# One block for norm and front, a 128-row step projection, silu(z) and gating moved forward, and two mixer batches joined

## The chip, the cores and the metric

The kernel runs on one core of a Trainium2 chip. The metric is the device time of one execution in microseconds (us). Engines are named as in the profile: PE (TensorE; PEld its weight loads), DVE (VectorE), ACT (ScalarE), POOL (GpSimd) and SP (SyncE, which issues the DMAs here). They run their own instruction streams in order and meet at semaphores.

## The reference

Four layers work on x, 1024 tokens (4 batches of 256) by 512 values, each with a layer norm before, a layer norm after and a residual add. They are a selective scan, a layer of experts with low-rank parts, a 128-head mixer with causal convolution, and a gated FFN. The change touches the first and the third. The first is, cut:

```python
proj = hidden_states @ in_proj_w            # 512 -> 2 x 1024
x, z = jnp.split(proj, 2, axis=-1)
xc = silu(conv4(x) + conv_b)                # causal, 4 taps
ssm_p = einsum('bdl,ed->ble', xc, x_proj_w) # 64 rows: 32 step, 16 B, 16 C
dt_r, Bm, Cm = (rmsnorm(part) for part in ssm_p)
dt = softplus(einsum('blr,dr->bdl', dt_r, dt_proj_w) + dt_bias)
ys = _selective_scan(xc, dt, -exp(A_log), Bm, Cm)
y = (ys + D_param[None, :, None] * xc) * silu(z)
return einsum('bdl,hd->blh', y, out_proj_w)
```

The third projects to 18,560 columns, convolves, and forms for each head and batch a kernel of decays times C.B products, which is multiplied with the head's values (two heads share a pair of 128 rows).

## The kernel before, in words

Stages follow one another as blocks; every engine meets the others at a block's end. Products of full precision are done as three fp32r matmuls of high and low parts (`mm3`, lines 78 to 80): high by high, high by low, low by high.

`first_norm` (L175) is the first block after the one that loads constants. SP loads the eight 128-token tiles of x; DVE waits for all of them, takes the statistics (L201, L204), and after ACT's root (L219) normalizes (L208). PE turns each tile (L230), ACT copies the high part (L222), DVE subtracts for the low part (L213).

`scan_front` (L234) is the second block. SP loads `w_in0` in eight slices of 256 columns (L280) and six tables (L286); POOL splits each slice (L300, L302). PE does 32 `proj` steps of 12 matmuls of 128x512 on three banks: the first 16 are x, two per 128 channels (one for each half of the tokens), the last 16 are z. An x step is followed by ACT's first tap (L441), three taps on DVE (L382), ACT's Silu (L447) and one `x_proj` matmul (L326) three steps later. A z step is copied by DVE (`z_copy`, L390). Once x is done, the 64 rows are squared (L457), summed by matmul (`sums`, L334), rooted (L460), inverted (L404) and scaled (L406). Then come 16 `steps` (L342), plain f32 matmuls of 32 rows on two banks, two between each pair of z steps. ACT takes Abs (L465) and Exp (L469) and, after all, Ln (L472); DVE takes the relu (L395) and the last sum (L433).

`selective_scan` (L475) runs 128 units in order: 8 `kk` (two channel tiles and one half of the tokens) of 16 states `n`. In a unit, PE makes the inputs (L689, 16 matmuls), ACT the decay (L551), DVE scans (L608), POOL multiplies by C (L645), PE sums over states two units later (L700, 8 matmuls). The ring of scanned tiles and that of products hold three each. At n = 8 of the next `kk` DVE adds the skip (`skip`, L616), at n = 9 it makes dt times x (L600), at n = 10 PE turns that (L659).

`out_proj_and_norm` (L721): ACT takes Silu of z in place in eight parts (L871), DVE multiplies it into y (`gated`, L932), ACT and DVE split y (L880, L937), ACT and POOL split the weights (L875, L791), and PE multiplies: four pairs of channel tiles, then four token tiles. `gated(6)` and `gated(7)` stand among the norm's statistics (L941 and on).

`mixer_groups` (L1374) runs eight groups of nine steps: step 0 of a group projects B and C, steps 1 to 8 each project a pair of heads (four `proj` of 12 matmuls, each in two parts), while PE does the pair before: it turns the pair's values (`turn`, L1612) and multiplies them with the kernels (`y_mm`, L1629 and L1633, one call per batch b = 0 to 3). Kernels are made by ACT (L1930, L1931 clamps; L1943, L1949 exponentials) and DVE (L1754), eight per pair in four buffers; `y_mm(p, 0)` frees two of them for kernels 4 and 5, `y_mm(p, 1)` for 6 and 7. Steps 1 to 4 of groups 1 to 7 also hold two `out_tile` calls of 24 matmuls each (outputs of the group before), whose input parts come from ACT (L1958) and DVE (L1795); steps 5 to 8 prepare weights for them (L1965, L1808).

PE's order within such a step is written by hand (L1673 on):

```python
turn(p, 0); proj(s, 0, 0); proj(s, 0, 1)
turn(p, 1); proj(s, 1, 0); proj(s, 1, 1)
y_mm(p, 0)
if outs: out_tile(*outs[0])
proj(s, 2, 0); proj(s, 2, 1)
y_mm(p, 1)
proj(s, 3, 0); proj(s, 3, 1)
if outs: out_tile(*outs[1])
y_mm(p, 2); y_mm(p, 3)
```

## Time and profile before

| | |
|---|---|
| Median of 3 runs | 2557.45 us (2557.25 to 2561.41) |
| The profiled execution | 2554.48 us, span 2552.7 us |
| Mean granted TensorE clock | 0.969 |
| Busy: PE, DVE, ACT, POOL | 93%, 72%, 59%, 48% of the span |

A busy share is that of instructions in execution, and PE's are pipelined, so a full PE row is not PE at its peak: what counts is the distance from one start to the next. A bracket behind an instruction is the idle time of its engine before it and what ended that. `x8` is a run of eight instructions of a kind.

### The profile page before, as it was taken

Reading aid. Unit: us, or ns where it says so; the run is one execution under the profiler, and the core shown is the slowest. Engines: PE = TensorE matmul, PEld = TensorE weight load, DVE = VectorE, ACT = ScalarE, POOL = GpSimd, SP = SyncE. Lnnn points to the kernel's source line nnn. Section 1 sums busy time; section 2 is a strip of 40 time slices with the busy share of each in tenths; the row PEclk is TensorE's granted clock in tenths of the full one; section 3 lists DMA queues with packets and bytes.
Section 4 is the critical chain, followed back from the end, with each engine's and each line's share of the span. In section 5 each row is a group of like instructions: output and inputs, shape, how many; then the busy total and the mean of one; then the engine's idle time right before and its main releaser. Section 6 shows DMA issues by size and latency. Waiting matters only on the chain. (4 is left out here: it accounts for less than half of the span.)

```text
span 2552.7 us, 38270 instructions
## 1 busy us (share of the span) xinstructions
PE 2371.1 (93%) x13836; PEld 1916.2 (75%) x13836; DVE 1840.2 (72%) x3052; ACT 1504.5 (59%) x3201; POOL 1213.3 (48%) x782
## 2 busy tenths in 40 slices
PE   5979999977669999999999999999999999779997
PEld 4559999976456777777777777777777777569996
DVE  4558888875548866966966857857857867697777
ACT  2365585553338956857857867857758668632221
POOL 1228888864224734634625724724635535432212
PEclk9989999998879999999999999999999999899999
DMA  2010020021023412312312213313223223201100
GB/s 83 26 67 2 1 67 1 1 71 34 34 86 107 124 50 82 116 51 82 111 54 94 97 58 99 96 53 102 90 66 99 80 64 100 90 26 50 47 30 34
DMA packets 108540, 167.42 MB, mean 66 GB/s; under 512 B 9488, under 2 KB 77456, under 8 KB 107328
## 3 DMA queue, kind: packets, MB, share of 16 engines
q1 hardware_dynamic: 108352, 164.97, 20.2%
q8 instruction: 111, 1.82, 0.3%
q14 instruction: 77, 0.63, 0.1%
HBM read 158.58 MB, written 6.36 MB: 65 GB/s over the span
## 5 line engine op out<-in xcount | busy, mean ns | idle before, releaser
L78 PE MATMUL mg_pb<-xTh,mg_wh 128*128 128x512 f32 x1152 | 479.5, 416 | 8.1 <-PEq L1296 8.1
L1544 POOL TENSOR_TENSOR mg_y<-mg_hT,mg_sg 128x512 f32<-128x512 f32 x128 | 187.7, 1467 | 598.1 <-DVE mg_hT L1779 598.1
L79 PE MATMUL mg_pb<-xTl,mg_wh 128*128 128x512 f32 x1152 | 454.0, 394 | 0.0
L80 PE MATMUL mg_pb<-xTh,mg_wl 128*128 128x512 f32 x1152 | 452.4, 393 | 0.0
L1727 DVE SCALAR_TENSOR_TENSOR mg_hT<-mg_pb,mg_cw,mg_hT 128x510 f32<-128x510 f32 (+2 forms) x432 | 319.0, 743 | 23.2 <-ACT mg_hT L1899 14.6
L608 DVE TENSOR_TENSOR_SCAN o<-ss_da,ss_dbx 128x1024 f32<-128x1024 f32 x128 | 291.7, 2284 | 51.8 <-PE ss_dbx L689 49.3
L1754 DVE TENSOR_TENSOR mg_m<-mg_gb,mg_cb 128x384 f32<-128x384 f32 x512 | 265.7, 550 | 71.5 <-ACT mg_gb L1949 68.2
L78 PEld LDWEIGHTS mg_pb<-xTh,mg_wh 128*128 128x128 f32 x1152 | 217.2, 189 | 67.2 <-issue 27.6
L689 PE MATMUL ss_dbx<-ss_diag,ss_uT 128*128 128x128 f32 x2048 | 253.0, 277 | 7.7 <-DVE o L608 6.9
L80 PEld LDWEIGHTS mg_pb<-xTh,mg_wl 128*128 128x128 f32 x1152 | 217.4, 189 | 51.3
L551 ACT ACTIVATE ss_da<-dt,ss_na 128x510 f32<-128x510 f32 x256 | 170.3, 714 | 144.6 <-DVE o L608 144.5
L689 PEld LDWEIGHTS ss_dbx<-ss_diag,ss_uT 128*128 128x128 f32 x2048 | 241.2, 194 | 10.2 <-DVE o L608 8.9
L79 PEld LDWEIGHTS mg_pb<-xTl,mg_wh 128*128 128x128 f32 x1152 | 218.0, 189 | 38.5
L645 POOL TENSOR_TENSOR ss_pr<-o,ss_c 128x1024 f32<-128x1024 f32 x86 | 206.4, 2400 | 35.9 <-PE ss_zT L700 32.9
L1949 ACT ACTIVATE mg_gb<-mg_nd 128x256 f32<-128x256 f32 x512 | 189.7, 371 | 54.7 <-DVE mg_nd L1772 54.7
L1943 ACT ACTIVATE mg_gb<-mg_abc,mg_tabs 128x128 f32<-128x128 f32 x512 | 183.2, 358 | 22.8 <-DVE mg_m L1754 21.9
L78 PE MATMUL mg_tb<-mg_wogh,mg_yh 128*128 128x512 f32 x448 | 180.0, 402 | 0.0
L1534 POOL TENSOR_TENSOR mg_wl<-mg_ws,mg_wh 128x1024 fp32r<-128x1024 f32 x71 | 175.1, 2466 | 5.9
L79 PE MATMUL mg_tb<-mg_wogl,mg_yh 128*128 128x512 f32 x448 | 177.1, 395 | 0.0
L80 PE MATMUL mg_tb<-mg_wogh,mg_yl 128*128 128x512 f32 x448 | 177.0, 395 | 0.0
L1629 PE MATMUL mg_py<-mg_m,mg_hc 128*64 128x256 f32 x1024 | 166.2, 403 | 9.2 <-DVE mg_m L1754 9.1
L1803 DVE SCALAR_TENSOR_TENSOR o<-mg_tb,mg_rs,o 128x512 f32<-128x512 f32 x56 | 41.8, 747 | 179.4 <-PE mg_tb L80 179.4
(323 smaller groups left out, 5370.4 us busy)
## 6 DMA issues: line engine op xcount, KB each, us to landing
mg_abc<-acs_rows SPq DMA_DIRECT2D x256, 256.0 KB, 3.4
mg_ws<-in_w_in SPq DMA_DIRECT2D x72, 512.0 KB, 3.7
mg_wos<-in_w_out SPq DMA_DIRECT2D x64, 256.0 KB, 3.7
ss_c<-c_rows SPq DMA_DIRECT2D x8, 1024.0 KB, 5.8
ff_ws<-in_w SPq DMA_DIRECT2D x7, 1024.0 KB, 4.9
x<-in_x SPq DMA_DIRECT2D x16, 256.0 KB, 4.4
ip_ws<-in_w_in SPq DMA_DIRECT2D x8, 512.0 KB, 3.5
ff_w2s<-in_w SPq DMA_DIRECT2D x7, 512.0 KB, 7.1
```

Source lines behind the costliest of these rows:

```text
L78: pe.matmul(out, lhs[0], rhs[0], start=start, stop=False)
L79: pe.matmul(out, lhs[0], rhs[1], start=False, stop=False)
L80: return pe.matmul(out, lhs[1], rhs[0], start=False, stop=stop)
L608: dve.tensor_tensor_scan(hh[i % RH], da[i % 2][:], dbx[i % 2][:], 0.0, ALU.mult, ALU.add).then_inc(s_h, 1)
L645: pool.tensor_tensor(pr[i % RP], two(hh[i % RH]), crow[:, n, :].unsqueeze(1).to_broadcast([P, 2, HALF]), ALU.mult).then_inc(s_pr, 1)
L689: ins = pe.matmul(dbx[i % 2][:, a * HALF + m * P:a * HALF + (m + 1) * P], uT[kk % 2][:, a, m, :], diag[:, n, m, :], start=True, stop=True)
L1534: pool.tensor_tensor(wl[s % 2][:], ws[:], wh[s % 2][:].bitcast(F32), ALU.subtract).then_inc(s_lo, 1)
L1544: pool.tensor_tensor(yb[:, p % RING, t], hT[s % 2][:, t], sg[s % 2][:, t], ALU.mult).then_inc(s_y2, 1)
L1727: i = dve.scalar_tensor_tensor(out=d3, in0=s3, scalar=w[:, TAPS - 1 - k:TAPS - k], in1=d3, op0=ALU.mult, op1=ALU.add)
L1754: dve.tensor_tensor(mm[u % 4][:], gb[u % 2][:, 0:BLK], cbt[:, u // 2, :], ALU.mult).then_inc(s_m, 1)
L1943: act.activation(gb[u % 2][:, 2 * P:BLK], abc[(BATCH * p + b) % 3][:, hh, P:SEQ], ACT.Exp, bias=tabs[g % 2][:, 2, 2 * b, 2 * q + hh:2 * q ...
L1949: act.activation(gb[u % 2][:, 0:2 * P], nd[u % 4][:], ACT.Exp, scale=1.0 if by_dve(p, b) else -1.0).then_inc(s_e, 1)
```

## The change

1. `first_norm` goes; its work is done inside `scan_front`'s block, in two halves of four token tiles. SP loads four tiles of x, the first weight slice, the other four tiles, the second slice, then seven tables. PE turns four tiles, does `proj(0)` (which needs the first half of the tokens only), turns the other four and goes on with `proj(1)`.
2. The step projection becomes one fp32r matmul of 128 rows. The rows are B, C and the 32 step rows three times; `x_proj` now gives 128 rows instead of 64. `bch` holds high parts, with low parts in the last 32 rows; `dph` holds the projection's high part, with its low part in rows 64 to 95. POOL makes `dph` before slice 4, ACT copies `bch` high (two Copy), DVE subtracts (two). `steps` uses four banks and goes in groups of four, each followed by one z step; the turning of B moves behind the first group.
3. z steps 0 to 8 leave their bank through ACT's Silu; z steps 9 to 15 are copied by DVE and get Silu in place at the block's end. All Exp come after all Abs.
4. Gating leaves `out_proj_and_norm`: POOL gates the `kk` before at n = 11 of `kk` 1 to 7 in the scan, DVE the last one after the last skip.
5. In the mixer `y_mm(p, 0)` and `y_mm(p, 1)` stand together, behind the first `out_tile` and ahead of `proj(s, 2, 0)`.

Core of the diff:

```diff
+    TH = MT // NH
+    Z_ACT, GROUP = 9, 4
...
+        dph = sb(c, "sp_dph", [R, DIN], F32R)
+        bch = sb(c, "sp_bch", [R, TOK], F32R)
+        dp, p0, sq = (sz[:, CD // 2 + i, :] for i in range(3))
-        pd = banks(c, "sp_pd", 2)
+        pd = banks(c, "sp_pd", 2) + pp
+        x = dt[:, 0:CD // 2, :].rearrange("p k (a d) -> p (k a) d", d=DM)
+        h0 = sz[:, 0:CD // 2, :].rearrange("p k (a d) -> p (k a) d", d=DM)
...
+                def load_x(h):
+                    for m in range(h * TH, (h + 1) * TH):
+                        sp.dma_start(x[:, m, :], x_tok[:, m, :]).then_inc(s_x[h], 16)
+                load_x(0)
                 load(0)
+                load_x(1)
                 load(1)
-                for t, n in ((cw, "conv_w0"), (cb, "conv_b0"), (xp, "x_proj"), (dp, "dt_proj"), (db, "dt_bias0"),
-                             (lw, "ln_w0")):
-                    sp.dma_start(t[:], I[n]).then_inc(s_tab, 16)
+                for t, n in ((cw[:], "conv_w0"), (cb[:], "conv_b0"), (xp[:], "x_proj"), (dp, "dt_proj"), (db[:], "dt_bias0"),
+                             (lw[:], "ln_w0"), (blk[:], "norm_blocks")):
+                    sp.dma_start(t, I[n]).then_inc(s_tab, 16)
...
+                def dt_weights():
+                    pool.wait_ge(s_tab, 112)
+                    pool.wait_ge(s_lo, 4)
+                    pool.tensor_scalar(dph[:], dp, 1.0, 0.0, ALU.mult, ALU.add).then_inc(s_dph, 1)
+                    pool.wait_ge(s_dph, 1)
+                    pool.tensor_tensor(dph[2 * RNK:3 * RNK, :], dp[2 * RNK:3 * RNK, :],
+                                       dph[2 * RNK:3 * RNK, :].bitcast(F32), ALU.subtract).then_inc(s_dph, 1)
+                    pool.wait_ge(s_dph, 2)
                 for s in range(CD):
+                    if s == 4:
+                        dt_weights()
...
+                def turn_x(m):
+                    pe.wait_ge(s_h0, m + 1)
+                    if m >= len(pd):
+                        pe.wait_ge(s_x0lo, m - len(pd) + 1)
+                    for k in range(KD):
+                        i = pe.transpose(pd[m % len(pd)][:, k * P:(k + 1) * P], h0[:, m, k * P:(k + 1) * P], ident)
+                    i.then_inc(s_t0, 1)
                 def proj(n):
...
+                    if n < 2:
+                        pe.wait_ge(s_x0lo, (n + 1) * TH)
                     if n >= 3:
-                        if n - 3 < NT:
+                        z = n - 3 - NT
+                        if z < 0:
                             pe.wait_ge(s_cv, n - 2)
+                        elif z < Z_ACT:
+                            pe.wait_ge(s_sz, z + 1)
                         else:
-                            pe.wait_ge(s_sz, n - 3 - NT + 1)
+                            pe.wait_ge(s_zc, z - Z_ACT + 1)
...
                 def steps(n):
                     k, h = divmod(n, 2)
-                    pe.wait_ge(s_bcn, h + 1)
-                    if n >= 2:
-                        pe.wait_ge(s_rl, n - 1)
-                    pe.matmul(pd[n % 2][:], dp[:, k * P:(k + 1) * P], bcn[0:RNK, half(h)], start=True, stop=True
+                    pe.wait_ge(s_bcl, h + 1)
+                    if n == 0:
+                        pe.wait_ge(s_dph, 2)
+                    if n >= len(pd):
+                        pe.wait_ge(s_rl, n - len(pd) + 1)
+                    elif n >= 2:
+                        pe.wait_ge(s_cp, n - 1)
+                    pe.matmul(pd[n % len(pd)][:], dph[:, k * P:(k + 1) * P], bch[:, half(h)], start=True, stop=True
                               ).then_inc(s_pd, 1)
...
+                for m in range(TH):
+                    turn_x(m)
+                proj(0)
+                for m in range(TH, MT):
+                    turn_x(m)
+                for n in range(1, NT):
                     proj(n)
...
-                done = 0
-                for n in range(NT + 5, 2 * NT):
-                    for i in range(done, min(done + 2, NT)):
+                for n in range(NT // GROUP):
+                    for i in range(n * GROUP, (n + 1) * GROUP):
                         steps(i)
-                    done = min(done + 2, NT)
+                    if n == 0:
+                        turn_b()
+                    proj(NT + 5 + n)
+                for n in range(NT + 5 + NT // GROUP, 2 * NT):
                     proj(n)
-                for i in range(done, NT):
-                    steps(i)
-                for m in range(MT):
-                    i = pe.transpose(pq[:, m * R:(m + 1) * R], bcn[:, m * P:(m + 1) * P], cst[0:R, C_ID:C_ID + R])
-                i.then_inc(s_bt, 1)
...
+                for h in range(NH):
+                    norm_x(h)
+                    for m in range(h * TH, (h + 1) * TH):
+                        x_low(m)
+                dve.wait_ge(s_tab, 112)
                 for n in range(NT):
                     taps(n)
-                z_copy(0)
                 copied(0)
-                z_copy(1)
                 copied(1)
-                z_copy(2)
                 normed(0)
                 normed(1)
-                z_copy(3)
-                z_copy(4)
-                done = 0
-                for n in range(5, NT):
-                    for i in range(done, min(done + 2, NT)):
-                        relu(i)
-                    done = min(done + 2, NT)
+                for h in range(NH):
+                    r = slice(3 * RNK, R)
+                    dve.wait_ge(s_bch, h + 1)
+                    dve.wait_ge(s_bcn, h + 1)
+                    dve.tensor_tensor(bch[r, half(h)], bcn[r, half(h)], bch[r, half(h)].bitcast(F32), ALU.subtract
+                                      ).then_inc(s_bcl, 1)
+                for n in range(NT):
+                    relu(n)
+                    if n == GROUP - 1:
+                        dve.wait_ge(s_bt, 1)
+                        dve.tensor_copy(bt[:], pq[:, 0:MT * RNK].rearrange("p (m r) -> p m r", r=RNK)[:, :, 0:NST]
+                                        ).then_inc(s_dt, 1)
+                for n in range(Z_ACT, Z_ACT + 4):
                     z_copy(n)
-                for i in range(done, NT):
-                    relu(i)
-                dve.wait_ge(s_bt, 1)
-                dve.tensor_copy(bt[:], pq[:].rearrange("p (m r) -> p m r", r=R)[:, :, RNK:RNK + NST]).then_inc(s_dt, 1)
-                for k in range(CD):
-                    dve.wait_ge(s_ln, k + 1)
-                    dve.tensor_tensor(dt[:, k, :], dt[:, k, :], rl(k), ALU.add).then_inc(s_dt, 1)
+                step_sum(0)
+                z_copy(13)
+                step_sum(1)
+                step_sum(2)
+                z_copy(14)
+                step_sum(3)
+                z_copy(15)
+                for k in range(4, CD):
+                    step_sum(k)
...
+                def z_silu(n):
+                    k, h = divmod(n, 2)
+                    act.wait_ge(s_proj, NT + n + 1)
+                    act.activation(sz[:, k, half(h)], pb[(NT + n) % 3][:], ACT.Silu).then_inc(s_sz, 1)
...
+                for h in range(NH):
+                    root_x(h)
+                    for m in range(h * TH, (h + 1) * TH):
+                        x_high(m)
...
                 silu(NT - 1)
-                for h in range(NH):
-                    act.wait_ge(s_cp, h + 1)
-                    act.activation(sq[:, half(h)], p0[:, half(h)], ACT.Square).then_inc(s_sq, 1)
+                z_silu(0)
+                squares(0)
+                z_silu(1)
+                squares(1)
+                z_silu(2)
...
+                for h in range(NH):
+                    act.wait_ge(s_bcn, h + 1)
+                    act.activation(bch[:, half(h)], bcn[:, half(h)], ACT.Copy).then_inc(s_bch, 1)
+                z_silu(3)
+                z_silu(4)
...
+                    act.activation(dt[:, k, half(h)], pd[n % len(pd)][:], ACT.Abs, bias=db[:, k:k + 1]).then_inc(s_abs, 1)
+                    if n % GROUP == GROUP - 1:
+                        z_silu(5 + n // GROUP)
...
+                    act.activation(dt[:, k, :], dt[:, k, :], ACT.Exp, scale=-1.0).then_inc(s_exp, 1)
+                for k in range(CD):
+                    act.wait_ge(s_exp, k + 1)
                     act.activation(dt[:, k, :], dt[:, k, :], ACT.Ln, bias=eps[:, 3:4]).then_inc(s_ln, 1)
+                for n in range(Z_ACT, NT):
+                    k, h = divmod(n, 2)
+                    act.wait_ge(s_zc, n - Z_ACT + 1)
+                    act.activation(sz[:, k, half(h)], sz[:, k, half(h)], ACT.Silu).then_inc(s_zs, 1)
...
                 skip(KB - 1)
-                dve.wait_ge(s_fin, 2 * KB)
+                for a in range(2):
+                    k = tiles(KB - 1).start + a
+                    dve.wait_ge(s_fin, 2 * KB - 1 + a)
+                    dve.tensor_tensor(xc[:, k, tokens(KB - 1)], xc[:, k, tokens(KB - 1)], sz[:, k, tokens(KB - 1)],
+                                      ALU.mult).then_inc(s_gv, 1)
+                dve.wait_ge(s_gv, 2)
...
+                    if n == GATE_AT and kk:
+                        xv = xc[:, tiles(kk - 1), tokens(kk - 1)]
+                        pool.wait_ge(s_fin, 2 * kk)
+                        pool.tensor_tensor(xv, xv, sz[:, tiles(kk - 1), tokens(kk - 1)], ALU.mult).then_inc(s_gp, 1)
...
-                silu(0)
-                silu(1)
-                for j in range(HT):
+                high(0)
+                weights_high(0)
+                high(1)
+                for j in range(1, HT):
                     weights_high(j)
-                    high(j)
-                    if j < 3:
-                        silu(2 * j + 2)
-                        silu(2 * j + 3)
+                high(2)
+                high(3)
                 high(4)
...
-                gated(0)
-                gated(1)
                 for j in range(HT):
                     low(j)
-                    gated(j + 2)
...
-                    if m < 2:
-                        gated(6 + m)
...
                         proj(s, 1, 0)
                         proj(s, 1, 1)
-                        y_mm(p, 0)
                         if outs:
                             out_tile(*outs[0])
+                        y_mm(p, 0)
+                        y_mm(p, 1)
                         proj(s, 2, 0)
                         proj(s, 2, 1)
-                        y_mm(p, 1)
                         proj(s, 3, 0)
```

## Rows read from the trace of the kernel before

**Rows 1.** Busy time of stages; columns: stretch, length, busy (instructions), clock, DMA, GB/s.
```profile
98.50:164.50 66.00, 64.54 (x231) 39.74 (x230) 32.32 (x38) 34.60 (x39) 6.85 (x4) 1.00 0.03 9
...
183.30:551.70 368.40, 355.89 (x3176) 352.66 (x3175) 310.77 (x151) 207.08 (x367) 306.97 (x128) 1.00 0.06 19
...
790.00:2190.00 1400.00, 1385.19 (x7324) 1052.33 (x7324) 1025.16 (x1831) 1024.30 (x2326) 687.02 (x489) 1.00 0.27 85
```
**Rows 2.** Timeline, first norm to first projection; columns: start, length, engine, line, instruction.
```profile
3.37 3.65 SPq L194 DMA_DIRECT2D x<-in_x  x8
...
12.27 4.85 DVE L201 BATCH_NORM_STATS2 n_st<-x 128x6 f32<-128x512 f32 x8 [11.32 <-DMA x<-in_x]
...
18.40 3.74 DVE L208 TENSOR_SCALAR n_h<-x,n_mv,n_rs 128x512 f32<-128x512 f32 x8
...
20.15 0.60 ACT L222 ACTIVATE xTh<-n_tb 128x512 fp32r<-128x512 f32 x1 [2.02 <-PE n_tb L230]
...
22.05 4.89 DVE L213 TENSOR_TENSOR xTl<-n_tb,xTh 128x512 fp32r<-128x512 f32 x8
...
34.32 0.80 PE L78 MATMUL ip_pb<-xTh,ip_wh 128*128 128x512 f32 x1 [9.02 <-POOL ip_wl L302]
```
**Rows 3.** Timeline of ACT, DVE and PE, second half of the front.
```profile
108.44 0.77 ACT L460 ACTIVATE sp_sq<-sp_pq,eps,cst 64x512 f32<-64x512 f32 x1 [1.30 <-PE sp_pq L334]
...
116.66 0.88 DVE L406 SCALAR_TENSOR_TENSOR sp_bcn<-sp_p,sp_lw,sp_sq 64x512 f32<-64x512 f32 x1
...
150.76 1.98 PE L342 MATMUL sp_pd<-sp_bcn,sp_dp 32*128 32x512 f32 x4
...
154.58 1.28 ACT L472 ACT_TABLE_LOAD   x1
...
155.87 8.43 ACT L472 ACTIVATE dt<-dt,eps 128x1024 f32<-128x1024 f32 x8
...
158.45 0.69 DVE L390 COPY sz<-ip_pb 128x512 f32<-128x512 f32 x1 [2.03 <-PE ip_pb L80]
...
169.27 4.63 DVE L433 TENSOR_TENSOR dt<-dt,sp_rl 128x1024 f32<-128x1024 f32 x4
```
**Rows 4.** Timeline of POOL and DVE, last units of the scan.
```profile
536.86 2.36 POOL L645 TENSOR_TENSOR ss_pr<-o,ss_c 128x1024 f32<-128x1024 f32 x1 [0.32 <-PE ss_zT L700]
...
541.23 2.29 DVE L608 TENSOR_TENSOR_SCAN o<-ss_da,ss_dbx 128x1024 f32<-128x1024 f32 x1 [0.37 <-PE ss_dbx L689]
```
**Rows 5.** Timeline of POOL and PE, output projection: its start, and one later wait.
```profile
557.14 2.34 POOL L791 TENSOR_TENSOR op_wl<-x,op_wh 128x1024 fp32r<-128x1024 f32 x1 [10.33 <-ACT op_wh L875]
...
560.71 0.76 PE L78 MATMUL op_b<-op_wh,op_yh 128*128 128x512 f32 x1 [10.49 <-DVE op_yl L937]
...
598.03 1.12 PE L852 MATMUL op_tb<-cst,o 128*128 128x128 f32 x4 [2.60 <-DVE o L961]
```
**Rows 6.** Timeline of DVE and PE, mixer, two kinds of step.
```profile
1115.96 1.29 DVE L1795 TENSOR_TENSOR mg_yl<-mg_y,mg_yh 128x256 fp32r<-128x256 f32 x2
...
1205.97 0.66 PE L1612 MATMUL mg_tb<-cst,mg_hT 128*128 128x128 f32 x4
...
1215.99 0.39 PE L80 MATMUL mg_pb<-xTh,mg_wl 128*128 128x512 f32 x1
...
1217.45 0.40 PE L79 MATMUL mg_pb<-xTl,mg_wh 128*128 128x512 f32 x1
...
1220.09 0.65 PE L1629 MATMUL mg_py<-mg_m,mg_hc 128*64 128x256 f32 x4
...
1220.79 0.60 PE L1629 MATMUL mg_py<-mg_m,mg_hc 128*64 128x256 f32 x4
...
1221.54 0.66 PE L1612 MATMUL mg_tb<-cst,mg_hT 128*128 128x128 f32 x4
...
1236.91 0.65 PE L1629 MATMUL mg_py<-mg_m,mg_hc 128*64 128x256 f32 x4 [0.37 <-DVE mg_m L1754]
...
1237.71 0.65 PE L1612 MATMUL mg_tb<-cst,mg_hT 128*128 128x128 f32 x4
```

182 lines of the change are left out of this document (85 added, 97 removed).

## The prediction, made before the change was run

> **What bounds the kernel now.** I read the busy times by stage first: PE is occupied for 1385 of the mixer's 1400 us, for 356 of 368 in the scan and for 64.5 of 66 in the second half of the front, all at the full clock level, 2.4 GHz [rows 1]. Then I read the timeline around each edited place. The start is different: PE waits until 34.32 for its first projection, behind one serial chain (x lands, statistics, root, normalize, turn, split, and only then the weights' own load and split) [rows 2]. At the front's end ACT is in its eight Ln until 164.30 and DVE in its last sums until 173.90, while PE has done its last z step [rows 3]. So the start and the end of the front are not PE's; nearly everything between is, and there an edit pays only if it shortens PE's list or a wait of PE.
>
> **1. Norm inside the front.** Eight x tiles are issued in 3.65 us from 3.37 and all are there at 12.27 [rows 2]. With four of them issued by 5.2, I take 8.6 for the first half (an estimate: half way between 3.37 and 12.27, plus 0.8 for what every load takes). From first statistic to first normalized tile eight tiles took 6.13 us (12.27 to 18.40), 4.85 of them statistics [rows 2]; four tiles save half of that and 0.3 of aggregates, so 3.4 us: 12.0. The first high part came 1.75 after that point (20.15 against 18.40 [rows 2]); the later ones follow PE's turns, 0.86 apart, and the low part ends 1.2 after its high part begins: the fourth is there at 12.0 + 1.75 + 2.6 + 1.2 = 17.6. Slice 0 is queued behind four tiles only and is split by then. So proj(0) starts near 17.8 instead of 34.32. But DVE works in order: the second half's statistics begin only at 17.7; 3.4 us to 21.1, four tiles normalized at 3.74/8 = 0.47 each by 23.0, four low parts of 4.89/8 = 0.61 [rows 2] from 23.2 to 25.7. proj(1) starts at 25.7 if PE turns at 2.4 GHz, at 27.4 if at 1.2; in before it followed proj(0), at 38.9. That is 11.5 to 13.2 us less. PE idles for about 1 us on each side of these turns, and the first 3.9 us of projection ran at the lower level in before; a new fall would cost 1 to 2 us. I take **-12.0**, ends -13.2 and -9.5. SP's queue is passed by nothing urgent: its two larger tables, 1.1 MB with the rest, stand behind slice 1 and are wanted at 26.
>
> **2. 128 rows in x_proj.** The 16 matmuls and two sums move the same 512 columns; only their weights have twice the columns. **+0.5**, ends 0 and +1.6 (0.1 each). POOL's extra pair before slice 4 (3.4 us) lies in its wait for PE, over 9 us for each slice: 0; without that cover it would delay proj(16) by 3.4.
>
> **3. Second half of the front.** Two f32 steps hold PE for 1.98 us [rows 3]. As fp32r they are two of the matmuls of which 12 make the 2.72 us (0.69 + 2.03) from one z copy to the next [rows 3], 0.227 each, so 16 steps shed 16 x 0.76 = 12 us of PE. What is late next, in the times of before: ACT must do z_silu(2), ready at 107.4, before it may load the root's table, so the first root starts 0.9 us after the 108.44 of [rows 3] and both inversions shift with it. The last scaling ends at 118.4 instead of 117.54 [rows 3]; then come one Copy and one subtraction of 0.6 each, so that steps 0 and 1 start at 119.2 and 120.0, and PE has idled 2.3 us. Behind these waits stand the z steps, and ACT's and DVE's queues behind theirs. The four groups are paced by PE (3.65 us) and by the relu (0.8 us each against four banks): z steps 5 to 8 end at 124.5, 128.7, 132.4 and 136.5, and seven more at 2.72 end at 155.5. ACT is last now: Silu 0.6, table 1.28, eight Exp 8.4, table 1.28, eight Ln 8.43 [rows 3], table 1.28, seven Silu 3.9: 136.6 + 25.2 = 161.8. DVE's sums (4.63 for four [rows 3]) end at 160.6. The block ended at 173.90: -12.1. If PE's level falls in the 2.3 us gap, as it did after 2.60 us idle, where four transposes took 1.12 us [rows 5], z step 5 and all behind it are up to 1.5 late. I take **-11.3**, ends -12.8 and -6.
>
> A table load is 1.28 us in the trace and the next ACT instruction starts 0.01 behind it (154.58, 155.87 [rows 3]). The Trainium skill, "ScalarE: Activation LUTs", What ACT_TABLE_LOAD costs, gives every switch a drain of about 1.38 us on top. By the page the three loads from the Exp on would end the block at 165.9 and the whole sum would be -21.4; this row shows no such gap.
>
> **4. Gates in the scan.** They are seven POOL instructions of the size of L645, 2.36 us [rows 4]. POOL repeats every 2.66, so the next product is up to 2.1 late and 0.3 is made good per unit. Behind it wait a scan (for the product three before) and PE's sum. Product 124 ended at 539.22 and scan 127 began at 541.23 [rows 4], a slack of 2.0; the sum comes later still. So a gate costs 0 to 0.2 in the middle, where I take 0 (2.36 each if the slack is gone). In the last `kk` only four units are left to catch up: 1.65 late. DVE's two gates come after the last skip, where nothing runs beside them: 2 x 0.65. Together **+2.95**, ends +1.3 and +17.8.
>
> **5. Output projection.** PE started at 560.71 on DVE's low part; the weights' low part was ready at 559.48 [rows 5]. Silu and gate are gone from in front of the first, the weights' load and split are not: **-1.1** (560.6 to 559.5), and the weights are late next. The two gates among the norm's statistics lay in DVE's waits for POOL: 0. Ends -3 and 0.
>
> **6. Mixer.** A lone y_mm costs 1.00 us: 1215.99 to 1217.45, less two matmuls of 0.23; the second of a pair costs 0.70, 1220.09 to 1220.79 [rows 6]. Joining sheds 0.30 of PE per pair of heads, 19.2 for 64. Not all of it counts. In the steps with weights (5 to 8) a loop of ACT exponentials, DVE kernels, taps and clamps back to ACT needs some 16.3 us. PE's own step is 15.57 (1205.97 to 1221.54); the next is 16.17, PE waiting 0.37 for DVE's kernel [rows 6]. What PE sheds in these steps it waits: 0. Steps 3 and 4, where PE never waits, save 0.6 per group, step 0 of the next group 0.3. Step 2 loses: `out_tile` comes first now and needs DVE's low part, ready at 1117.25 [rows 6], while PE arrives at 1116.7: +0.55 - 0.30. That is -0.65 per group and **-4.5** for seven. In the steps with outputs y_mm(p, 0) comes 5.6 us later, so kernels 4 and 5 start about 2 us later, and queued behind them on DVE is the low part of the second output tile: 1128.7 instead of 1126.7 in the step of these rows, still 1.2 us before PE wants it. Ends -19.2 and +10.
>
> **Sum.** -12.0 + 0.5 - 11.3 + 2.95 - 1.1 - 4.5 = -25.5. The profiled execution took 2554.5, 3.0 under the median of 2557.45, so 2529.0 in a profile and 2532.0 as a median.
>
> **The rivals.**
> A, 0.16: the new front waits more. PE's level falls in both gaps and the relu paces the groups: +3 and +3, 2538. For it: the new path passes ACT, DVE and PE twice. Against: most of PE's work there is covered by ACT's last 25 us.
> B, 0.10: the mixer pays every join, -19.2 instead of -4.5: 2517. For it: PE is idle for 1.1% of the stage [rows 1]. Against: the 0.37 [rows 6].
> C, 0.07: each gate stalls the scan in full, +16.5: 2548. Against: the slack of 2.0 [rows 4].
> D, 0.06: ACT's table loads hold more than their row; once more 1.28 for each of three is 3.8: 2536. It is the way of the page named above, and the row speaks against it.
> E, 0.05, the other side: in the 21 steps with outputs DVE's second low part comes after PE. Beyond its 1.2 us of slack each microsecond costs 21. All other parts give -21, so it turns the sum when the low part comes 2.2 us later than I count and is measurably slower from 2.45: at 2.5 it is 2563. Against: PE does 5.5 us of projection between kernel 5 and that tile.
> The forecast holds 0.56.
>
> **How the numbers follow.** The forecast's own spread is 2524 to 2540. With A, D and half of B the range is 2517 to 2545, 0.83 of the cases. About 0.2%, 5 us, can be told from no change. Slower is E beyond its point, 0.03; same is E's milder part, 0.02; all else is faster, 0.95.
>
> **What would show it.** proj(0) near 18, proj(1) near 26; the front's block ending near 150 with ACT's Silu last; step matmuls 0.23 apart and PE idle over 2 us before the first; scan units 2.66 apart after each gate; PE's first output matmul 1.9 us later behind the last scan; mixer steps 5 to 8 as long as before and steps 3 and 4 shorter by 0.3. It is wrong if the front saves under 18 us, if a gate opens a gap in PE, or if PE waits for a low part in every step with outputs.

## The result, and the profile after

The changed kernel takes **2521.61 us** (median of 4 runs, 2520.92 to 2523.64) where the kernel before took 2557.45 (4 runs as well; the table ahead says 3). The ratio is 0.9857, with a 95% interval from 0.9842 to 0.9871: 35.8 us less. In the profiled execution the span is 2519.0 us instead of 2552.7, 33.7 less. The forecast was 2532.0 with a range from 2517 to 2545. So the direction and the range were right, and the gain was 10 us larger than forecast, by misses of both signs, the largest of them in the mixer and around `x_proj`.

The page of the changed kernel, its first part:

```profile
span 2519.0 us, 38251 instructions
PE 2339.3 (93%) x13820; PEld 1925.9 (76%) x13820; DVE 1823.6 (72%) x3040; ACT 1511.1 (60%) x3213; POOL 1232.6 (49%) x791
```

The shares are those of before. Where the time went is seen only from places that both kernels have. The table has the start of the same instruction in both traces, and the shift so far; a difference between two shifts is what a stage gained in this pair of profiles.

| Place | Before | After | Shift | Stage gained | Forecast |
|---|---|---|---|---|---|
| proj(1), first matmul | 38.9 | 30.19 | -8.7 | -8.7 | -12.0 |
| first `sums` matmul | 107.33 | 93.67 | -13.7 | -5.0 | +0.5 |
| ACT's first table load of the scan | 174.39 | 149.31 | -25.1 | -11.4 | -11.3 |
| end of DVE's last work of the scan | 551.67 | 529.95 | -21.7 | +3.4 | +2.95 |
| output projection, first matmul | 560.71 | 537.96 | -22.75 | -1.0 | -1.1 |
| first `turn` of the mixer | 762.49 | 739.06 | -23.4 | -0.7 | 0 |
| last pair's `turn` in the mixer | 2190.53 | 2156.84 | -33.7 | -10.3 | -4.5 |
| span | 2552.7 | 2519.0 | -33.7 | 0 | 0 |

Each column is one profile, and the same code does not stand at the same place in each. a_step1 (below) moved no instruction and so repeats the changed kernel: there proj(1) starts at 27.70, the first `sums` at 91.14, the table load at 148.73 and the mixer's first `turn` at 738.89. So the first row could as well read -11.2 and the third -9.5, while the second (63.44 us from proj(1) to the first `sums` instead of 63.48) and the mixer's stay to 0.2. The kernel before varies too: in b_join, whose edit lies behind them, the table load comes at 178.58 and the first `turn` at 769.35, 4.2 and 6.9 later than in the table.

Busy time of the stages of the changed kernel that answer to [rows 1]: second half of the front, scan, mixer. Columns: stretch, length, then busy time and instructions of PE, PE's loads, DVE, ACT and POOL, the granted clock, DMA share, GB/s.

```profile
85.50:144.00 58.50, 53.62 (x215) 40.68 (x214) 31.19 (x36) 40.42 (x53) 7.18 (x5) 0.94 0.04 11
158.20:530.00 371.80, 356.97 (x3176) 353.42 (x3175) 311.88 (x153) 207.24 (x367) 321.78 (x135) 0.99 0.06 19
760.00:2156.00 1396.00, 1371.34 (x7340) 1058.91 (x7338) 1027.27 (x1835) 1032.32 (x2335) 689.38 (x491) 1.00 0.28 86
```

PE now idles for 5 of 58.5 us in the front's second half (before 1.5 of 66), with a clock of 0.94, and for 25 of 1396 us in the mixer (before 15 of 1400). Part of the work that was taken from PE has become waiting.

**The start.** Timelines of the changed kernel, answering to [rows 2]: DVE and POOL, then PE's first two projections. Columns as in [rows 2].

```profile
8.87 2.47 DVE L390 BATCH_NORM_STATS2 n_st<-dt 128x6 f32<-128x512 f32 x4 [7.92 <-DMA dt<-in_x]
11.34 2.34 POOL L275 TENSOR_TENSOR ip_wl<-ip_ws,ip_wh 128x1024 fp32r<-128x1024 f32 x1
12.34 5.76 DVE L397 TENSOR_SCALAR sz<-dt,n_mv,n_rs 128x512 f32<-128x512 f32 x4
15.41 2.40 POOL L275 TENSOR_TENSOR ip_wl<-ip_ws,ip_wh 128x1024 fp32r<-128x1024 f32 x1
20.77 0.77 PE L78 MATMUL ip_pb<-xTh,ip_wh 128*128 128x512 f32 x1 [1.50 <-DVE xTl L403]
30.19 0.50 PE L78 MATMUL ip_pb<-xTh,ip_wh 128*128 128x512 f32 x1 [1.90 <-DVE xTl L403]
```

The statistics start at 8.87, where 8.6 was estimated, and normalizing at 12.34, where 12.0 was. But the four TENSOR_SCALARs take 5.76 us; eight of them took 3.74 in [rows 2]. The line's own view says that it is single ones that are long:

```profile
L397 DVE TENSOR_SCALAR sz<-dt,n_mv,n_rs x8: 533/548/2565, 12.3 to 25.4; 128x512 f32<-128x512 f32 x8
```

(columns: duration in ns, least, median and most). Their stretch is the one in which POOL makes the low parts of weight slices 0 and 1. In five profiles of this code (a_step1, a_step2, a_lastgate and a_warm beside this one; their edits lie further on or move nothing) the four take 4.67 to 6.51 us and proj(1) starts at 27.70 to 30.83.

**The x steps.** PE's weight loads around one `x_proj`, first in the kernel before, then in the changed one:

```profile
82.71 0.19 PEld L326 LDWEIGHTS sp_pp<-xc,sp_xp 128*64 128x64 f32 x2 [0.35 <-issue]
83.71 0.19 PEld L78 LDWEIGHTS ip_pb<-xTh,ip_wh 128*128 128x128 f32 x1 [0.81 <-issue]
```

```profile
81.72 0.41 PEld L312 LDWEIGHTS sp_pp<-xc,sp_xp 128*128 128x128 f32 x2
82.37 0.19 PEld L78 LDWEIGHTS ip_pb<-xTh,ip_wh 128*128 128x128 f32 x1 [0.24 <-issue]
```

With 64 columns the load unit stands idle for 0.35 us ahead of the pair and for 0.81 behind it; with 128 columns the load comes right behind the one before it, and 0.24 is left behind the pair. The distance between two `x_proj` fell from 3.95 to 3.62 us. It is not a matter of 64 columns alone. In the kernel before the step matmuls have 128 weight columns but 32 rows, and the load unit stands idle around them too:

```profile
121.60 0.29 PEld L342 LDWEIGHTS sp_pd<-sp_bcn,sp_dp 32*128 32x128 f32 x2 [0.35 <-issue]
...
123.51 0.19 PEld L78 LDWEIGHTS ip_pb<-xTh,ip_wh 128*128 128x128 f32 x1 [0.76 <-issue]
```

**The second half of the front.** Timelines of PE, ACT and DVE in the changed kernel, answering to [rows 3]:

```profile
105.55 1.46 PE L332 MATMUL sp_pd<-sp_bch,sp_dph 128*128 128x512 f32 x2 [2.27 <-DVE sp_bch L448]
113.17 0.63 PE L332 MATMUL sp_pd<-sp_bch,sp_dph 128*128 128x512 f32 x2
...
124.40 0.60 ACT L496 ACTIVATE sz<-ip_pb 128x512 f32<-128x512 f32 x1 [0.76 <-PE ip_pb L80]
125.02 1.28 ACT L534 ACT_TABLE_LOAD   x1
126.31 7.70 ACT L534 ACTIVATE dt<-dt 128x1024 f32<-128x1024 f32 x8
...
145.07 3.75 ACT L541 ACTIVATE sz<-sz 128x512 f32<-128x512 f32 x7
...
144.05 4.62 DVE L413 TENSOR_TENSOR dt<-dt,sp_rl 128x1024 f32<-128x1024 f32 x4
```

PE waits 2.27 us ahead of the first step matmul (2.3 was forecast). Two of them then take 1.46 us where later pairs take 0.63; part of that is a wait of the second for DVE's second subtraction, since a_warm and a_port2, in which the clock stayed up, still needed 1.16. The first group lasts 7.62 us (105.55 to 113.17), later ones 3.7. ACT's Silu ends the block.

**The scan's end.** Timelines of POOL, PE and DVE in the changed kernel:

```profile
518.36 4.65 POOL L722 TENSOR_TENSOR ss_pr<-o,ss_c 128x1024 f32<-128x1024 f32 x2
523.07 1.09 PE L782 MATMUL ss_zT<-cst,ss_pr 128*128 128x128 f32 x8 [1.21 <-POOL ss_pr L722]
525.34 1.97 PE L750 MATMUL ss_tz<-cst,ss_u 128*128 128x128 f32 x8 [1.18 <-ACT ss_u L637]
528.67 1.28 DVE L707 TENSOR_TENSOR xc<-xc,sz 128x512 f32<-128x512 f32 x2
```

The last product ends 1.3 us late against the start of the scan, the last turning of y takes 1.97 us (1.09 before), and the two gates 1.28.

### The profile page after: what moved, and what is told of

It reads as the page before. It is cut to its first block and busy times, and to the rows that moved or that the text cites. A ratio compares the mean times of both kernels' runs of the same rounds, so it can differ in the third digit from the quotient of the medians.

```text
span 2519.0 us, 38251 instructions
## 1 busy us (share of the span) xinstructions
PE 2339.3 (93%) x13820; PEld 1925.9 (76%) x13820; DVE 1823.6 (72%) x3040; ACT 1511.1 (60%) x3213; POOL 1232.6 (49%) x791
## 5 line engine op out<-in xcount | busy, mean ns | idle before, releaser
L78 PE MATMUL mg_pb<-xTh,mg_wh 128*128 128x512 f32 x1152 | 471.8, 410 | 8.0 <-PEq L1363 8.0
L722 POOL TENSOR_TENSOR ss_pr<-o,ss_c 128x1024 f32<-128x1024 f32 x86 | 206.3, 2405 | 26.9 <-PE ss_zT L782 23.9
L1966 ACT ACTIVATE mg_hT<-mg_pb,mg_cbias,mg_cw 128x512 f32<-128x512 f32 x144 | 110.5, 768 | 77.9 <-PE mg_pb L80 73.7
```

The lines of the kernel that those rows point to most:

```text
L78: pe.matmul(out, lhs[0], rhs[0], start=start, stop=False)
L722: pool.tensor_tensor(pr[i % RP], two(hh[i % RH]), crow[:, n, :].unsqueeze(1).to_broadcast([P, 2, HALF]), ALU.mult).then_inc(s_pr, 1)
```

## The experiments

Each kernel is one of the two with the edit shown; its name stands in brackets.

**The mixer's order alone (b_join).** In the kernel before:

```diff
-                        y_mm(p, 0)
                         if outs:
                             out_tile(*outs[0])
+                        y_mm(p, 0)
+                        y_mm(p, 1)
                         proj(s, 2, 0)
                         proj(s, 2, 1)
-                        y_mm(p, 1)
```

> The kernel before with one edit: y_mm(p, 0) and y_mm(p, 1) stand together behind the first out_tile, as in the changed kernel. Theory J: all of the mixer's 10.3 us comes from this order alone. So the time falls by 10.3 (9 to 12): groups 1 to 7 by 4.1 together, and group 0 by 6.1, its third and fourth steps from 19.99 and 18.11 to 16.0 and 16.3, because POOL's weight split no longer runs beside DVE's clamps. Rival K: group 0 was shortened by something that came in from the stages ahead (when its loads and splits start against PE), so the order alone gives the groups' 4.1 and group 0 keeps a step near 20: 3.5 to 5 us less.

Measured: 2549.0 against 2558.26 for the kernel before on the same chip, 9.3 less (ratio 0.9962, 0.9947 to 0.9977), within the 9 to 12 expected. In its profile the mixer, from the first pair's turn to the last one's, took 9.6 us less than before. The third and fourth pair of group 0 took 16.01 and 16.35 (19.99 and 18.11 before), groups 1 to 7 together 3.5 less. Theory J holds: the order brings nearly all of the mixer's gain, group 0's too. (The profile's span, 2550.0, is only 2.7 under that of before, because the unchanged code ahead of the mixer took 6.9 longer in it.)

**Why two steps of group 0 were long (b_nosplit).** In the kernel before:

```diff
+                    c0 = slice(0, 1) if s in (4, 5) else slice(0, 2 * P)
-                    pool.tensor_tensor(wl[s % 2][:], ws[:], wh[s % 2][:].bitcast(F32), ALU.subtract
-                                       ).then_inc(s_lo, 1)
+                    pool.tensor_tensor(wl[s % 2][:, :, c0], ws[:, :, c0], wh[s % 2][:, :, c0].bitcast(F32),
+                                       ALU.subtract).then_inc(s_lo, 1)
```

> The kernel before (mixer order as it was), in which POOL's low part of the mixer's weights for steps 4 and 5 is made for one column of 256 only, so these two instructions take well under 1 us instead of 2.4; the other columns keep old values, the output is wrong by that, and nothing else is changed. They are the two splits that lie beside DVE's clamps in the two long steps of group 0 (19.99 and 18.11 us, one clamp 2.37 us where 0.28 is usual). Theory P: a POOL instruction and a DVE instruction that both work on SBUF hold each other up, and these two splits are why the steps are long. Then the clamps take 0.3 to 1.1, the two steps fall to 16.0 to 17 and the time by 4 to 5.5. Rival O: the steps are long because of the order of y_mm (the kernels of p are freed late) and the clamps are only late with them; then the steps stay within 0.5 of 19.99 and 18.11 and the time within 1.

Measured: the steps took 16.39 and 16.68, and the time 2552.76 against 2561.08, 8.3 less (ratio 0.9971, 0.9962 to 0.9981), where 4 to 5.5 were expected. The two steps gave 5.0 and the rest of the mixer 0.1; its profile's span is 4.0 under that of before. The 3 us between 5.0 and 8.3 are not explained. Timelines of DVE, POOL and PE in the kernel before, then of DVE and POOL in this one:

```profile
780.88 2.39 POOL L1534 TENSOR_TENSOR mg_wl<-mg_ws,mg_wh 128x1024 fp32r<-128x1024 f32 x1
780.99 2.37 DVE L1772 TENSOR_SCALAR mg_nd<-mg_abc,mg_tabs 128x128 f32<-128x128 f32 x1
784.11 0.63 PE L1612 MATMUL mg_tb<-cst,mg_hT 128*128 128x128 f32 x4 [2.68 <-DVE mg_hc L1745]
```

```profile
782.14 0.25 POOL L1535 TENSOR_TENSOR mg_wl<-mg_ws,mg_wh 128x4 fp32r<-128x4 f32 x1
782.24 0.28 DVE L1773 TENSOR_SCALAR mg_nd<-mg_abc,mg_tabs 128x128 f32<-128x128 f32 x1
```

In the kernel before, a clamp of 0.28 us starts 0.11 behind POOL's split and ends 0.09 behind it. The second long step has the same pair (800.56 and 800.67). PE waits 2.68 us for what stands next in DVE's queue. With a short split the same clamp takes 0.28. The steps had been long because of POOL and DVE, not because of PE's order; the order decides when POOL's gated product is released, and so, it seems, where the split behind it lies; b_join shows the effect, not each link of that chain.

**The width of x_proj alone (b_xp128).** In the kernel before:

```diff
-        xp = sb(c, "sp_xp", [P, CD, R])
+        xp = sb(c, "sp_xp", [P, CD, 2 * R])
-                    i = pe.matmul(pp[h][0:R, :], xp[:, k, :], xc[:, k, half(h)], start=k == 0, stop=k == CD - 1)
+                    i = pe.matmul(pp[h][:], xp[:, k, :], xc[:, k, half(h)], start=k == 0, stop=k == CD - 1)
-        "x_proj": f("L0_attn_x_proj_w").T.reshape(CD, P, -1).transpose(1, 0, 2),
+        "x_proj": np.concatenate(2 * [f("L0_attn_x_proj_w")]).T.reshape(CD, P, -1).transpose(1, 0, 2),
```

> The kernel before with one edit: the 64 weight columns of x_proj are loaded twice, so each of the 16 matmuls has 128 weight columns; the second 64 rows of its output are never read. Theory W: a 64-column f32 weight load isn't started ahead of time, PE pauses 0.35 us before it and 0.81 before the next one, and with 128 columns both pauses shrink. So the distance from one x_proj to the next falls from 3.95 to 3.62, and the time by 5.3 (4.5 to 6). Rival S: the pauses belong to the switch between f32 and fp32r whatever the width, and the changed kernel's x steps got shorter through something else (the first weight slices being ready, ACT's order). Then the distance stays 3.95 or grows by up to 0.1, and the time changes by 0 to +1.6.

Measured: 3.6 us less (2554.64 against 2558.26; ratio 0.9984, 0.9975 to 0.9993), under the 4.5 to 6 expected, though the interval reaches into them. PE's loads in this run:

```profile
83.69 0.42 PEld L326 LDWEIGHTS sp_pp<-xc,sp_xp 128*128 128x128 f32 x2
84.35 0.19 PEld L78 LDWEIGHTS ip_pb<-xTh,ip_wh 128*128 128x128 f32 x1 [0.24 <-issue]
```

They are those of the changed kernel, and the distance between two `x_proj` is 3.60. From proj(1) to the first `sums` it took 63.57 us instead of 68.45, 4.9 less, which is the whole of the -5.0 in the table. All of it was lost again ahead of the mixer in this one profile (first `turn` at 762.56, before 762.49), within what the same code varies by; the gain in time is read from the medians. Theory W holds for the distance: doubling the columns of this matmul made it cheaper, and the switch between f32 and fp32r, which both kernels have, is not the price. What in the chip holds back a load that does not fill 128 rows and 128 columns, no run here shows. The loads of `y_mm`, 128x64, also have a pause ahead of them (0.36 at 1220.09 in the kernel before), and the second of a joined pair has none, so the 0.30 that a join saves may be of the same kind. The Trainium skill, "TensorE: Matmul & The Clock Gate", Step-by-step: what each phase is for, has weight loads pulled ahead of running matmuls when their row groups don't conflict or the load goes to the background buffer, and their time grow with the columns. The second agrees (136 ns for 64 columns, 188 for 128); the loads of 64 columns were not pulled ahead here, and no run shows which of the two conditions they missed.

**Keeping POOL's split off the normalization (a_splitwait).** In the changed kernel:

```diff
                     pool.wait_ge(s_hi, s + 1)
+                    if s == 0:
+                        pool.wait_ge(s_h0, TH)
                     pool.tensor_tensor(wl[q][:], ws[q][:], wh[q][:].bitcast(F32), ALU.subtract).then_inc(s_lo, 1)
```

> The changed kernel with one more wait: POOL makes the low part of weight slice 0 only after DVE has normalized the first four tiles. Theory P: DVE's normalizing TENSOR_SCALARs and POOL's split hold each other up (four took 5.76 us in the changed kernel, up to 2.57 for one, where eight took 3.74 before). With the wait the four take 2.0 us, the weights' low part is ready at 16.6, proj(0) starts at 17.7 instead of 20.77 and proj(1) at 26 instead of 30.19: 4 us less (3 to 4.5). Rival L: the four are slow because of their new source and destination tiles or of x still arriving; then they still take 5.8, the low part of slice 0 comes at 20.5, proj(0) at 20.8 or later, and the time is the same or up to 2 us longer.

Measured: 2520.05 (2518.9 to 2522.73), 1.6 under the changed kernel's median. That is less than the 3 to 4.5 expected, and the runs overlap with the changed kernel's, so by the time alone no gain is shown. Timelines of DVE, PE and POOL:

```profile
12.27 1.92 DVE L399 TENSOR_SCALAR sz<-dt,n_mv,n_rs 128x512 f32<-128x512 f32 x4
18.05 0.76 PE L78 MATMUL ip_pb<-xTh,ip_wh 128*128 128x512 f32 x1 [1.50 <-DVE xTl L405]
26.33 0.50 PE L78 MATMUL ip_pb<-xTh,ip_wh 128*128 128x512 f32 x1 [1.90 <-DVE xTl L405]
...
99.58 2.37 POOL L277 TENSOR_TENSOR ip_wl<-ip_ws,ip_wh 128x1024 fp32r<-128x1024 f32 x1
100.14 2.36 DVE L431 SCALAR_TENSOR_TENSOR sp_bcn<-sz,sp_lw 128x512 f32<-128x512 f32 x1
```

Theory P holds for the cause: the four take 1.92 instead of 5.76 us (1.92 in all five kernels with this wait), and proj(0) starts at 18.05 and proj(1) at 26.33, 0.25 and 0.63 behind the forecast. But the gain of 3.9 us there shrank to 2.0 at the scan's start: the split of slice 6 lay beside DVE's second scaling, which took 2.36 instead of 0.75. The new wait was not what brought them together. a_step1, the changed kernel without it, has the same pair:

```profile
100.93 2.37 POOL L275 TENSOR_TENSOR ip_wl<-ip_ws,ip_wh 128x1024 fp32r<-128x1024 f32 x1
101.50 2.35 DVE L429 SCALAR_TENSOR_TENSOR sp_bcn<-sz,sp_lw 128x512 f32<-128x512 f32 x1
```

POOL's pair of instructions for slice 6 waits for PE. It began 7.05 us behind the first `sums` in the changed kernel's profile, where the granted clock behind the second `sums` was 1.00 (96.67 to 98.67), and 8.65 behind in a_step1 and a_splitwait, where it was 0.67 (94.14 to 96.14) and 0.61 (92.79 to 94.79). So PE's fall to the lower level made POOL late, and POOL then held up DVE. b_join shows the same in the kernel before (clock 0.61, the scaling 2.48 instead of 0.88).

**Moving that hold-up (a_port, a_port2).** Two waits, tried in turn, each added to the edit above. The first:

```diff
+                    if s == 6:
+                        pool.wait_ge(s_bcn, 2)
```

> The changed kernel with two waits for POOL: the low part of weight slice 0 comes after DVE's first normalization, as in a_splitwait, and that of slice 6 after both inversions of the step, B and C rows. Theory P: in a_splitwait 3.9 us were won at proj(1) and 1.6 of them lost again when the split of slice 6 lay beside DVE's second scaling (2.36 us instead of 0.75). With the second wait the scaling takes 0.75, the first step matmul comes at 101.7 instead of 103.28 (105.55 in the changed kernel) and the front ends 3.5 to 4 us ahead of the changed kernel's. Rival C: what was lost there was lost to PE's clock, which fell in the same stretch; then the step matmuls come at 103 still, and the time is that of a_splitwait.

Measured: 2519.31. The scaling takes 0.75 again, but the split now started with DVE's next instruction, the subtraction for the low rows:

```profile
101.96 2.78 POOL L279 TENSOR_TENSOR ip_wl<-ip_ws,ip_wh 128x1024 fp32r<-128x1024 f32 x1 [1.57 <-DVE sp_bcn L433]
101.84 3.44 DVE L452 TENSOR_TENSOR sp_bch<-sp_bcn,sp_bch 32x512 fp32r<-32x512 f32 x2
105.34 0.79 PE L336 MATMUL sp_pd<-sp_bch,sp_dph 128*128 128x512 f32 x1 [2.26 <-DVE sp_bch L452]
```

Two subtractions of 32 rows took 3.44 us instead of 1.35, and PE waited 2.26 for the second. Neither theory had this. By the time it is 2.3 less than the changed kernel, with runs from 2517.55 to 2520.24. The second has `s_bcl` in place of `s_bcn`:

> The changed kernel with two waits for POOL: slice 0's low part comes after DVE's first normalization, slice 6's low part after DVE's two subtractions for the low parts of the step rows (in a_port it came one instruction earlier and the hold-up moved onto the first of these two, 3.44 us for both instead of 1.35). Theory P: no critical DVE instruction lies beside a split any more. The scaling takes 0.75 and the two subtractions 1.35; the four step matmuls come without the gap of 2.26, the first at 102 against 105.55 in the changed kernel, and the front ends 3 to 4 us earlier (the time 2 to 4 us less, since PE's clock may take some back). Rival C: PE's clock in the waits ahead of the steps sets that stretch; then the front ends at most 2 us earlier, as in a_splitwait.

Measured: 2517.41 (2517.09 to 2517.69), 4.2 under the changed kernel; ratio to before 0.9827 (0.9812 to 0.9842).

```profile
101.74 1.35 DVE L452 TENSOR_TENSOR sp_bch<-sp_bcn,sp_bch 32x512 fp32r<-32x512 f32 x2
102.49 0.50 PE L336 MATMUL sp_pd<-sp_bch,sp_dph 128*128 128x512 f32 x1 [0.70 <-DVE sp_bch L452]
```

The first step comes at 102.49 (105.55 in the changed kernel), and the mixer begins 4.2 earlier; all four runs are faster than any of the changed kernel's. Not all of it is the splits' doing. PE's wait ahead of the first step was only 0.70, the clock stayed at 1.00 behind it, and the first group took 5.0 us instead of 7.62, so the block ended 5.5 earlier (3 to 4 were expected), of which the scan's start took 1.4 back. Theory P and rival C each have a part in this run. The Trainium skill, "SBUF — State Buffer", Who interferes with whom, says that a DVE instruction in a two-port mode, which TENSOR_SCALAR can take, and a GpSimd instruction lock each other out of shared ports, and that whoever issues first has them for the whole instruction. It says that a DVE instruction with two inputs in SBUF contends with a GpSimd instruction that reads SBUF. Four places agree: TENSOR_SCALARs of 2.57 for 0.53 and 2.37 for 0.28, and with two inputs 2.36 for 0.75 and 3.44 for 1.35.

**PE's clock ahead of the steps (a_warm).** In the changed kernel, nine matmuls of 128x512 that nothing reads, in PE's wait:

```diff
+                def warm(bank, n):
+                    for i in range(n):
+                        pe.matmul(bank[:], xT[0][:, 0, 0:P], xT[0][:, 0, half(0)], start=True, stop=True)
...
+                    if n == 0:
+                        warm(pd[0], 9)
                     for i in range(n * GROUP, (n + 1) * GROUP):
                         steps(i)
```

> The changed kernel with nine more matmuls of 128x512 on PE, 2.1 us together, in its wait of 2.27 us ahead of the first step matmul; they write a bank whose content is overwritten, and nothing reads it. Theory C: PE's clock falls to the lower level in that wait, and the first group of step matmuls, the turning of B and the z step behind it take 7.6 us (105.55 to 113.17) where 4.2 would do at full clock. With PE busy the clock stays, the group takes 4.2 to 4.6, and the front ends 2.5 to 3.4 us earlier, because ACT's Exp, Ln and Silu start right behind the last group. Rival A: the 7.6 us are set by ACT and DVE emptying the four banks; then the group takes 7 or more, and the time stays within 0.5 or gets 0.2 longer.

Measured: 2519.75 (2517.19 to 2521.47), 1.9 less by the medians. Two runs lie near 2517.6 and two near 2521.45, inside the changed kernel's, so the gain is not clear. The profiled run is one of the slower two, 0.6 longer in span than the changed kernel's. PE's timeline, and the granted clock in a stretch of the scan (columns as above):

```profile
103.73 2.20 PE L344 MATMUL sp_pd<-xTh 128*128 128x512 f32 x9
111.21 0.62 PE L332 MATMUL sp_pd<-sp_bch,sp_dph 128*128 128x512 f32 x2
...
168.00:171.00 3.00, 3.00 (x17) 3.00 (x17) 2.31 (x2) 1.57 (x3) 1.06 (x2) 0.54 0.00 0
```

The first group took 5.0 us (106.19 to 111.21) instead of 7.62: theory C holds for the cause. In this profile the gain didn't reach the end: at the scan's start the clock fell in a stretch in which the changed kernel had 1.00, and again at its end.

**The last gate (a_lastgate).** In the changed kernel:

```diff
-                    if n == GATE_AT and kk:
+                    if i == UNITS - 1 or n == GATE_AT and 0 < kk < KB - 1:
```

> The changed kernel with POOL's last gate moved from state 11 of the last kk to behind the last product of the scan, where POOL is idle. Theory G: the gate delays the last products by 1.3 us, and the longer wait let PE's clock fall for the last turn (1.97 us instead of 1.09). The time falls by 1.3 to 2.2, with the last product of POOL ending 1.3 earlier against the scan's start. Rival H: the tail is set by DVE and PE and the gate fits in the slack; then the last product still ends as now and the time stays within 0.3.

Measured: 2521.29 (2517.5 to 2523.47), no difference that the runs show. In the profile POOL's last product comes 1.3 us earlier against the scan's start, as G says; PE's clock then fell one instruction sooner, the last sum took 1.87 us instead of 1.09, and 0.5 is left.

**y_mm ahead of the first out_tile (a_step1, a_step2).** The changed kernel, with an edit meant for the first step that has both outputs and a pair:

```diff
-                        if outs:
+                        first = bool(outs) and outs[0][1] == 0
+                        if outs and not first:
                             out_tile(*outs[0])
                         y_mm(p, 0)
                         y_mm(p, 1)
+                        if first:
+                            out_tile(*outs[0])
```

> The changed kernel, in which the first step with outputs of each group has y_mm(p, 0) and y_mm(p, 1) ahead of its first out_tile instead of behind it; the other steps are as changed. Theory D: that out_tile waits 0.44 to 0.6 us for DVE's low part, and the two y_mm can be done in that wait. So this step falls from 26.95 to 26.35 or 26.4, in 7 groups by 4 us, of which steps 5 to 8 give nothing back only if DVE and ACT are as early as PE; from 15.11 to 15.89 in step 5 in the changed kernel I expect half to be given back: 2 us less (0 to 4). Rival R: the kernels 2 and 3 aren't ready so early; PE waits for DVE there as long as it did for the low part, and the time stays within 0.5.

Measured: 2521.67. The condition names a step without a pair of heads, so no instruction moved. The run is a repeat of the changed kernel (2520.38 to 2523.16), and its median is 0.06 us from that one's, while its profile shows how far single places move (see the table above). With `== 2` it names the step that was meant:

> The changed kernel, in which the first step of a group that has both a turned pair and outputs takes y_mm(p, 0) and y_mm(p, 1) ahead of its first out_tile (a_step1 named a step that has no pair, so it changed nothing and repeated the changed kernel). Theory D: PE's wait of 0.44 for DVE's low part is filled by the two y_mm, whose kernels are ready; the step falls from 26.95 to 26.4 in seven groups, and since steps 5 and 6 wait for DVE's kernels they give back half or more: 0 to 3 us less, likeliest 1.5. Rival R: kernels 2 and 3 come no earlier than the low part, or all is given back in step 5: within 0.5 of the changed kernel.

Measured: 2535.67, **14.1 us more**. Theory D was wrong; R had the order right, since kernels 2 and 3 come later than the low part, but not the price. PE's timeline in such a step, and the row of the changed kernel for the wait that was to be filled:

```profile
1092.87 0.65 PE L1696 MATMUL mg_py<-mg_m,mg_hc 128*64 128x256 f32 x4 [2.03 <-DVE mg_m L1824]
```

```profile
1087.30 0.50 PE L78 MATMUL mg_tb<-mg_wogh,mg_yh 128*128 128x512 f32 x1 [0.44 <-DVE mg_yl L1862]
```

y_mm(p, 1) needs kernels 2 and 3, which DVE makes behind both low parts and the clamps; PE waits 2.03 us for them, and the step takes 28.4 to 30.0 us instead of 26.9 to 27.0, in seven groups. In the changed kernel the out_tile's 5.6 us of matmuls cover that: the join is worth something because it stands behind the out_tile.

**All together (best, best2).** The edits of a_port2, a_lastgate and a_warm, first with the order of a_step2 as well:

> The changed kernel with the edits of a_port2, a_step2, a_lastgate and a_warm together. If their effects add: front 3.5 for the splits and 2.5 for the clock of the first group of steps, scan tail 0.5, mixer 1.5, so 8 us less than the changed kernel, 2513 to 2514. If PE's clock falls somewhere else for what it is spared here (as a_warm lost 1.2 at the scan's start), 2515 to 2518.

Measured: 2530.44, the forecast broken by that order. The 739.1 in the next text is the first `y_mm`; the mixer's first `turn` came at 732.64 (739.06 in the changed kernel). Without the order:

> The changed kernel with the edits of a_port2, a_lastgate and a_warm, and the mixer as changed. In the run of best, which also had a_step2's order, the mixer began 6.5 us earlier than in the changed kernel (739.1 against 745.6) and then lost 14 by that order. If the mixer is set by its own order alone and doesn't care when it begins, this kernel is 6.5 us ahead of the changed one: 2515 (2514 to 2517). The rival, that what is won ahead of the mixer is lost again in it or behind it (PE's clock), gives 2518 to 2520.

Measured: **2514.69** (2514.29 to 2515.58), 6.9 less than the changed kernel; ratio to before 0.9828 (0.9815 to 0.9842). This beats both kernels by the medians; the ratio's interval touches that of the changed kernel (0.9842), since the kernel before varies more on the chips than these do. The mixer began 6.4 us earlier and took as long as in the changed kernel. Against a_port2 it is 2.7 less by the medians, but the two ran on different chips and their ratios to before are the same (0.9827 and 0.9828), so what a_lastgate and a_warm add to a_port2 is not shown.

## Why the prediction was right, point by point

**1. Norm inside the front: -12.0, measured -8.7.** The chain was right to 0.4 us up to the start of the first normalized tile. The failed step is "four tiles normalized at 3.74/8 = 0.47 each": they took 5.76 us, because POOL split the weights beside them. The prediction had no term for POOL and DVE holding each other up. In [rows 2] no POOL instruction lies beside DVE's eight. a_splitwait put back what the step had assumed, and proj(0) and proj(1) came at 18.05 and 26.33 where 17.8 and 25.7 were forecast. The end of the range for this term, -9.5, didn't reach far enough either, since it was made for the clock alone. In a_step1 the four took 4.67 and the term was -11.2, so the size of this miss changes from run to run (0.8 to 3.3) and its cause does not.

**2. 128 rows in x_proj: +0.5, measured -5.0.** This is the term that was wrong in sign, and outside its own bounds of 0 and +1.6. "The same 512 columns" was the step: it counted the moving side and put the pauses around each load of 64 columns at nothing. b_xp128 showed that widening the load removes 0.35 us per `x_proj`, with nothing else changed. The lower end of the range, 0, left out a saving without giving a reason.

**3. Second half: -11.3, measured -11.4.** The first step came at 105.55, which is 119.2 in the times of before, as forecast. PE's clock fell in the wait, as named (granted 0.65 from 104.67 to 106.67, then 0.50), and z step 8's Silu began at 124.40 (138.06 in those times), 1.5 behind the forecast's 136.5, as named too. The fixed chain of ACT behind it was 0.8 shorter than counted. The table loads hold no more than their row (125.02, 1.28, then Exp at 126.31), so rival D is out in this kernel, and with it the drain that the Trainium skill, "ScalarE: Activation LUTs", What ACT_TABLE_LOAD costs, adds to a load. The agreement to 0.1 is partly luck: in a_step1, the same code, the stage gave -9.5, because POOL held up the second scaling as in a_splitwait, which the prediction did not foresee.

**4. Gates: +2.95, measured +3.4.** In the middle nothing: from the first sum of the scan to the last took 354.3 us against 353.0, all of it at the end (1.3; 1.65 was forecast). The gates on DVE cost 1.28. What was missing is 0.9 for the last turning at the lower clock (0.50 from 526 to 530). a_lastgate took the 1.3 away and got no clear time for it.

**5. Output projection: -1.1, measured -1.0.** The wait is now for POOL's low weights, as forecast (537.96, 10.66 of idle ended by L872). The working set out from 560.6 where its row has 560.71, a slip of 0.1. Another 0.7 came further on, for which the sum had no term. It is no more than the same code varies by: from the first output matmul to the mixer's first `turn` it took 201.8 us before, 201.1 in the changed kernel and 201.6 in a_step1.

**6. Mixer: -4.5, measured -10.3.** For groups 1 to 7 the working was right: 4.1 us less in the changed kernel, with steps 3 and 4 shorter by 0.36, the first output step longer by 0.3, and steps 5 to 8 giving back 0.5 of what PE had won. The failed step is one that wasn't made: the sum is "for seven" groups and puts group 0 at nothing without a reason, though its third and fourth steps stood in the trace of before with 20.0 and 18.1 us beside 15.6 and 16.3. They gave 5.8, because POOL's split no longer lay beside DVE's clamps (b_nosplit, b_join). That the order of PE's calls would move it there was not foreseen by any part of the prediction.

Rival A came true in its cause for one of its two gaps, and cost the 1.5 us named in step 3, not its 6. Rival B, every join paid, did not: 10.3 isn't its 19.2, and 5.8 of the 10.3 are DVE's and POOL's, not PE's. C had a full stall of each gate, and none was seen. E, the low part late in every step with outputs, did not come, but a_step2 shows how near such an order is to losing: 14 us from one misplaced pair of calls.

The total was no further off because misses of +3.3, -5.5, +0.5, -0.7 and -5.8 partly cancelled. That is partly luck: three of the six terms had the right size, and the two largest misses came from effects that the prediction did not have.

## What to carry to other kernels

When DVE's short SBUF instructions lie on the path, look at what POOL does in the same stretch of the timeline, and treat a duration taken from a stretch without POOL as a lower bound. A step that is longer than its neighbours for no reason in the code is a gain waiting for any edit that shifts the engines against each other; explain it before counting. Take two profiles of the same kernel before you read a stage's gain of 1 or 2 us from one pair: here the same code moved by 2.5 us at one place. And place a joined matmul behind work that covers the engine that feeds it.
